# Attention maxima: turned by VectorE and laid out by two transfers instead of transposed by TensorE, with a new order of steps

## The chip, the cores and the metric

The kernel runs on one core of a Trainium2 chip. The core has TensorE (matrix products, written to PSUM), VectorE, ScalarE and GpSimd (element-wise work), SyncE (which here only asks for transfers), and 16 DMA engines that move data between DRAM and SBUF. The metric is the device time of one execution in microseconds (us); less is better.

## The reference

Four transformer layers act one after the other on x, 16 samples of 256 tokens by 256 features, in float32. Layers 0, 2 and 3 are whole: self attention, cross attention to a context of 120 rows, and an MLP. Layer 1 has cross attention alone. All have 16 heads of 16 features. The part that matters here is the softmax inside each attention:

```
def _attend(q, k, v):
    attn = jnp.einsum('bhnd,bhsd->bhns', q, k) * SCALE
    attn = jax.nn.softmax(attn, axis=-1)
    o = jnp.einsum('bhns,bhsd->bhnd', attn, v)
    B, _, N, _ = q.shape
    return o.transpose(0, 2, 1, 3).reshape(B, N, D)
...
x = x + g_sa * x_sa          # self attention, projected and gated
x = x + x_ca                 # cross attention
h = jax.nn.gelu(xm @ fc1_w + fc1_b, approximate=True)
x = x + g_ff * x_ff          # MLP
```

A softmax needs the maximum of every row of scores (one for each query and head) before the exponentials.

## The kernel before

Everything of x stays in SBUF. A job is one part of a layer for one sample, and is cut into steps. A list of words gives the order in which all engines go through the steps: a word such as `F.S0` names a part and a step, and each engine, in its own in-order queue, does what its part of each step is and waits on semaphores for the rest. A step with `.d` marks where VectorE (and GpSimd and SyncE) take their share when it isn't at TensorE's place.

The parts: P makes q, k and v of a self attention, F is the self attention, A its projection; R makes q, k and v of a cross attention, G is the cross attention, B its projection; E is the MLP. A leading `1` is layer 1; `p`, `f`, `c`, `e` are the same parts for another sample. A turn handles each part once, each for another sample (`AHEAD`). Turns 3 to 21 follow `WITH_L1` and also hold layer 1's cross attention (its G steps in turns 6 to 21, 16 jobs); turns 22 to 46 follow `TURN` and are called plain turns here. `START` and `TAIL` are the first and last stretch. There are 48 self attentions and 64 cross attentions, 112 in all.

One attention goes like this. `S` steps (four for F, two for G) write scores with queries on the partitions into `score`, a tile of four PSUM banks of which there is only one, and VectorE reduces each to row maxima (L978). `X` is VectorE's: it writes the negated maxima in two parts, a rounded one and its remainder, into `max_parts` (L987, L990), 8 used columns in each 32. `M` turns them: TensorE transposes the two 128 by 128 tiles into a slot of the ring (three PSUM banks shared by all projections, transposes and MLP steps; called from L1294, recorded at L1144), and ScalarE copies them to `max_t` (L1106). `T` steps write the scores again, keys on the partitions (L1309), add the negated maxima by a product with the selector `sel` (L1314), and ScalarE takes exponentials (L1117). `PV` multiplies by v (L1340) and `O` turns and normalizes on VectorE (L1000 to L1011). Every S and every T must wait until the one before it has left `score`.

In a timeline `score<-k_G,q_G` is an S step of a cross attention, `score<-q_F,k_F` with `score<-max_t_F,sel` a T step of a self attention, `ring<-ident,max_parts_G` is M, `w_proj` is A.PR, `w_cp` or `room` with `o_t_B` is B.PR, `w_fc,h_t` is F20 or F21 of E.

Of the kernel before, what the change touches and what calls it, by code (L numbers as in the profile page):

```python
# [47 lines left out]

TURN = """
F.S0 f.O1 f.PV3 E.H0  # L50
F.S1 P.V E.RES E.H1 P.V.d
F.S2 P.LN E.H2
F.S3 E.H3 p.N P.gld A.PR F.X A.PR.d
G.S0 F.M B.PR B.PR.d R.C
G.S1 E.F20a E.F20b G.X
F.T0 E.F20b.d R.N P.Q e.N G.M R.A
F.T1 e.A p.A P.Q.d P.K F.PV0
G.T0 c.NC P.RES F.PV1 P.K.d
P.ld R.LN e.LN F.O0 R.RES G.O0
G.T1 E.gld c.AC P.ST R.KV R.KV.d E.F21a G.O1 G.PV0  # L60
F.T2 R.Q G.PV1
F.T3 E.F21b E.F21b.d F.PV2 R.Q.d c.ld
""".split()
WITH_L1 = """
F.S0 f.PV3 E.H0
F.S1 1R.C P.V P.V.d P.LN
F.S2 P.gld E.H1 f.O1 E.H2
F.S3 F.X 1R.LN E.RES E.H3
1G.S0 A.PR F.M A.PR.d
1G.S1 1G.X B.PR E.F20a  # L70
G.S0 E.F20b 1G.M B.PR.d
G.S1 E.F21a
1G.T0 1R.RES E.F20b.d P.Q e.N
1G.T1 R.N e.A P.Q.d 1G.PV0 R.RES G.X 1G.O0 P.K
F.T0 E.F21b 1G.PV1
F.T1 G.M F.PV0 P.K.d R.A
P.ld 1R.Q E.F21b.d
G.T0 F.PV1 1G.O1 R.C p.N p.A 1R.KV 1R.Q.d F.O0
G.T1 G.PV0 1R.KV.d G.O0 R.LN 1B.PR 1p.N 1p.NC
F.T2 G.PV1 G.O1 R.Q E.gld R.Q.d P.RES  # L80
F.T3 R.KV P.ST 1p.AC 1R.ld 1B.PR.d F.PV2 c.ld 1p.A R.KV.d e.LN
# [3 lines left out]
W0.v Z0.ZT Z0.ZC P0.N P0.ld P0.A Z0.ZM Z0.ZX W0.cpb W0.proj Z0.ZL P0.LN Z0.ZA W0.raw Z1.ZL P2.ld W0.fc1 P0.Q  # L85
P1.ld W0.self P0.Q.d Z1.ZA P0.K Z0.ZS0 P0.K.d Z1.ZC Z2.ZL Z2.ZA W0.cross P1.N Z0.ZG Z1.ZM Z1.ZX
F0.S0 P1.A
F0.S1 P0.V P0.V.d
F0.S2 P1.LN Z0.ZS1 Z2.ZC
F0.S3 Z2.ZG Z3.ZL Z2.ZS1 F0.X Z2.ZM Z2.ZX F0.M  # L90
F0.T0 P2.N Z3.ZC R0.ld P1.Q Z3.ZA P1.Q.d F0.PV0
F0.T1 P1.K Z2.ZS0
F0.T2 P1.K.d Z3.ZM F0.PV1 P1.V
F0.T3 P3.ld F0.PV2 F0.O0 Z3.ZG
F1.S0 W0.fc2 R0.C P1.V.d
F1.S1 P5.ld P2.A F0.PV3 W0.v2
F1.S2 F0.O1
F1.S3 P2.LN P0.RES P0.gld F1.X A0.PR A0.PR.d F1.M
F1.T0 R0.N Z3.ZX R0.RES P2.Q P2.Q.d R1.ld
F1.T1 P2.K R0.A P3.N R0.LN P2.K.d F1.PV0 P2.V F1.PV1  # L100
F1.T2 Z3.ZS1 R0.Q P2.V.d
F1.T3 F1.O0 R0.KV P3.A
F2.S0 P1.RES W1.l1 F1.PV2 R2.ld R0.KV.d W0.cp
F2.S1 R0.Q.d
F2.S2 F1.PV3 F1.O1
F2.S3 A1.PR F2.X P4.ld
# [2 lines left out]
F2.T0 G0.X P1.gld R1.C P3.Q G0.M
F2.T1 P3.K  # L110
G0.T0 R1.N P3.Q.d P3.K.d R1.A F2.PV0 R1.LN F2.PV1 P4.N
G0.T1 F2.O0 R1.Q G0.O0 G0.PV0
F2.T2 Z3.ZS0 R1.Q.d G0.O1 P2.RES G0.PV1
F2.T3 P4.A R1.KV R1.KV.d R1.RES R3.ld P2.gld F2.PV2
# [1285 lines left out]
```

## Time and profile before

| | us |
|---|---|
| median of 3 runs | 2577.09 |
| lowest and highest | 2574.03, 2577.36 |
| the profiled execution | 2577.71 |
| its span, first to last instruction | 2575.9 |
| TensorE busy | 2479.3 |
| VectorE busy | 1858.5 |
| ScalarE busy | 1274.0 |
| GpSimd busy | 467.2 |

Busy times are sums over the whole span; an engine that is busy for less may still be the one that another waits for at a given place. The granted clock is TensorE's share of its full speed.

### The profile page before, as it was taken

Reading aid. Unit: us, or ns where it says so; the run is one execution under the profiler, and the core shown is the slowest. Engines: PE = TensorE matmul, PEld = TensorE weight load, DVE = VectorE, ACT = ScalarE, POOL = GpSimd, SP = SyncE. Lnnn points to the kernel's source line nnn. Section 1 sums busy time; section 2 is a strip of 40 time slices with the busy share of each in tenths; the row PEclk is TensorE's granted clock in tenths of the full one; section 3 lists DMA queues with packets and bytes.
Section 4 is the critical chain, followed back from the end, with each engine's and each line's share of the span. In section 5 each row is a group of like instructions: output and inputs, shape, how many; then the busy total and the mean of one; then the engine's idle time right before and its main releaser. Section 6 shows DMA issues by size and latency. Waiting matters only on the chain.

```text
span 2575.9 us, 66165 instructions
## 1 busy us (share of the span) xinstructions
PE 2479.3 (96%) x27466; PEld 1848.3 (72%) x27466; DVE 1858.5 (72%) x3532; ACT 1274.0 (49%) x1810; POOL 467.2 (18%) x510
## 2 busy tenths in 40 slices
...
GB/s 188 129 93 78 78 74 74 74 80 87 83 77 76 90 81 96 77 101 68 56 76 74 56 76 74 62 96 78 80 107 60 82 84 78 78 66 80 82 33 42
DMA packets 236749, 207.56 MB, mean 81 GB/s; under 512 B 87682, under 2 KB 222020, under 8 KB 236452
## 3 DMA queue, kind: packets, MB, share of 16 engines
...
## 4 chain that ended last, share of the span: by engine, by line
PE 79%; DVE 12%; issue 3%; ACT 3%; SPq 2%; DMA 1%; POOL 1%; DVEq 0%; POOLq 0%; ACTq 0%
PE o_acc L1340 11%; PE score L1287 10%; PE ring L1371 10%; PE ring L1248 10%; PE ring L1362 10%; PE score L1309 8%; PE ring L1352 6%; DVE row_max_F L978 5%; DVE row_max_G L978 5%; PE ring L1144 4%; PE ring L1256 3%; PE score L1314 3%; PE ring L1268 2%; ACT probs L1117 2%; PE ring L1271 2%
## 5 line engine op out<-in xcount | busy, mean ns | idle before, releaser
L1117 ACT ACTIVATE probs<-score 120x2048 f32<-120x2048 f32 (+1 forms) x320 | 601.6, 1880 | 374.8 <-PE score L1314 368.0
L978 DVE TENSOR_REDUCE row_max_F<-score 128x8 f32<-128x2048 f32 x192 | 438.7, 2285 | 103.3 <-PE score L1287 102.8
L1371 PE MATMUL ring<-w_fc,h_t 128*128 128x256 f32 x1536 | 368.9, 386 | 1.0 <-ACT h_t L1128 1.0
L1362 PE MATMUL ring<-x_t_E,w_fc 128*128 128x256 f32 x1536 | 368.3, 386 | 0.0
L978 DVE TENSOR_REDUCE row_max_G<-score 128x16 f32<-128x1920 f32 x128 | 276.1, 2157 | 116.8 <-PE score L1287 116.8
L1128 ACT ACTIVATE h_t<-ring,cols 128x256 f32<-128x256 f32 x384 | 160.7, 470 | 341.1 <-PE ring L1362 341.0
L1362 PEld LDWEIGHTS ring<-x_t_E,w_fc 128*128 128x128 f32 x1536 | 280.8, 190 | 59.3 <-issue 20.3
L1000 DVE STREAM_TRANSPOSE o_turned<-o_acc 128x512 f32<-128x512 f32 x224 | 159.9, 714 | 220.3 <-PE o_acc L1340 220.3
L1371 PEld LDWEIGHTS ring<-w_fc,h_t 128*128 128x128 f32 x1536 | 282.5, 190 | 46.3 <-ACT h_t L1128 1.4
L1340 PE MATMUL o_acc<-probs,v_self 128*17 128x256 f32 x3072 | 204.3, 384 | 0.0
L793 POOL TENSOR_TENSOR x<-x,gated 128x256 f32<-128x256 f32 x96 | 70.3, 733 | 723.1 <-DVE gated L1032 723.1
L1248 PE MATMUL ring<-x_t_P,w_qk 128*128 128x256 f32 x768 | 197.8, 403 | 1.2 <-ACT x_t_P L1068 1.2
L1309 PE MATMUL score<-q_F,k_F 32*128 32x256 f32 x3072 | 166.6, 303 | 8.9 <-ACT probs L1117 5.7
L1309 PEld LDWEIGHTS score<-q_F,k_F 32*128 32x128 f32 x3072 | 119.3, 184 | 75.2 <-issue 55.7
L1248 PEld LDWEIGHTS ring<-x_t_P,w_qk 128*128 128x128 f32 x768 | 143.9, 197 | 35.2 <-issue 8.4
L1287 PEld LDWEIGHTS score<-k_F,q_F 32*128 32x128 f32 x3072 | 106.4, 188 | 84.2 <-DVE row_max_F L978 42.0
L1287 PE MATMUL score<-k_F,q_F 32*128 32x256 f32 x3072 | 146.3, 307 | 21.4 <-DVE row_max_F L978 18.5
L1287 PEld LDWEIGHTS score<-k_G,q_G 32*128 32x128 f32 x4096 | 125.3, 187 | 52.4 <-DVE row_max_G L978 28.0
L1287 PE MATMUL score<-k_G,q_G 32*128 32x120 f32 x4096 | 142.9, 277 | 14.8 <-DVE row_max_G L978 12.0
L787 POOL TENSOR_TENSOR x<-x,gated 128x512 f32<-128x512 f32 x48 | 60.8, 1267 | 423.0 <-DVE gated L1019 423.0
L1340 PE MATMUL o_acc<-probs,v_ctx 120*17 120x256 f32 x2048 | 135.5, 382 | 0.0
L1099 ACT ACTIVATE q_parts<-ring,cols 128x256 fp32r<-128x256 f32 x224 | 94.0, 472 | 80.9 <-PE ring L1248 78.9
...
## 6 DMA issues: line engine op xcount, KB each, us to landing
q_G<-q_parts SPq DMA_DIRECT2D x256, 128.0 KB, 2.1
q_F<-q_parts SPq DMA_DIRECT2D x192, 128.0 KB, 2.1
k_F<-k_parts SPq DMA_DIRECT2D x96, 256.0 KB, 2.5
k_F<-k_parts SPq DMA_DIRECT2D x192, 128.0 KB, 2.2
k_G<-k_parts SPq DMA_DIRECT2D x128, 120.0 KB, 2.2
k_G<-k_parts SPq DMA_DIRECT2D x256, 60.0 KB, 1.9
gate_now_P<-gate_rows SPq DMA_DIRECT2D x48, 256.0 KB, 3.2
gate_now_E<-gate_rows SPq DMA_DIRECT2D x48, 256.0 KB, 3.4
```

The costliest lines, as they stand in the source:

```text
L978: nc.vector.tensor_reduce(dst, src, AX.X, ALU.max).then_inc(row_max_ready[r].sem, 1)
L1000: nc.vector.transpose(o_turned[:, :, :, :].rearrange("p i b d -> p (i b d)"), o_acc[:, :])\
L1117: nc.scalar.activation(probs[v % 2][0:keys, :, :], score[0:keys, :].rearrange("p (h q) -> p h q", h=2 * GROUPS), ACT.Exp, scale=SCALE).the ...
L1128: last = nc.scalar.activation(h_t[:, c, :], ps[:, c % 2 * NT:(c % 2 + 1) * NT], ACT.Gelu_apprx_tanh, bias=col(m, "fc1", c))
L1144: return nc.tensor.transpose(dst, src, ident[0:rows_in, 0:rows_in])
L1248: last = mm(ps[:, c * NT:(c + 1) * NT], weight[:, k, at + c * P:at + (c + 1) * P], buffer(x_t, r, m, n)[:, k, :], start=k == 0, stop=k == ...
L1287: last = mm(score[:, col0:col0 + width], q_now[at, c, e, tile * P:(tile + 1) * P].bitcast(F32R), k_now[at, two, c, e, :].bitcast(F32R), st ...
L1309: mm(score[0:keys, g * BANK + e * NT:g * BANK + (e + 1) * NT], k_now[at, two, c, e, tile * P:tile * P + keys].bitcast(F32R), q_now[at, c, ...
L1340: last = mm(o_acc[32 * j:32 * j + HD + 1, i * NT:(i + 1) * NT], v_head, probs[v % 2][0:keys, 2 * j + i, :], start=tile == 0 and (i == 0 or ...
L1352: last = mm(ps[:, t * D:(t + 1) * D], buffer(o_t, r, m, n)[:, k, t * P:(t + 1) * P], weight[:, k, :], start=k == 0, stop=k == KC - 1)
L1362: last = mm(ps[:, c % 2 * NT:(c % 2 + 1) * NT], w_fc1[:, k, c * P:(c + 1) * P], buffer(x_t, r, m, n)[:, k, :], start=k == 0, stop=k == KC - 1)
L1371: last = mm(ps[:, 0:D], h_t[:, k, t * P:(t + 1) * P], w_fc2[:, k, :], start=k == 0, stop=k == MC - 1)
```

## The change

M is no longer a step of TensorE and ScalarE. `max_parts` is packed (64 columns for both tiles instead of 256, no zeros between). X gets a third operation on VectorE, which turns `max_parts` in squares of 32 by 32 into `max_turned`. Then GpSimd asks for two transfers: one in X, from `max_turned` to a DRAM tensor `max_rows` of 32 rows by 256 queries, and one in M, from there to all four groups of 32 partitions of `max_t`. T waits for the second. The selector's ones stand at another row in each group, since each group now holds all 32 rows. M doesn't take a ring slot any more, so that the slots of all later steps shift.

```
+        max_rows = {r: nc.dram_tensor(f"max_rows_{r}", [32, NT], F32, kind="Internal").ap() for r in "FG"}
...
-        max_parts = {r: sb(f"max_parts_{r}", [P, TT, P]) for r in "FG"}
+        max_parts = {r: sb(f"max_parts_{r}", [P, TT, GROUPS, PAIRS, 2]) for r in "FG"}
+        max_turned = {r: sb(f"max_turned_{r}", [P, TT, 32]) for r in "FG"}
...  (GpSimd)
+                elif step == "X":
+                    pool.wait_ge(max_turned_ready[r].sem, max_turned_ready[r].after(m, n))
+                    if max_laid[r].order[m, n] > 0:
+                        pool.wait_ge(max_laid[r].sem(m, n), max_laid[r].after(m, n) - 16)
+
+                    pool.dma_start(max_rows[r].rearrange("h (t a q) -> a h t q", t=TT, a=4), max_turned[r][:, :, :])\
+                        .then_inc(max_written[r].sem(m, n), 16)
+                elif step == "M":
+                    pool.wait_ge(max_written[r].sem(m, n), max_written[r].after(m, n))
+                    t_psum[r].wait_before(pool, m, n)
+                    pool.dma_start(max_t[r][:, :], max_rows[r].unsqueeze(0).to_broadcast([GROUPS, 32, NT]))\
+                        .then_inc(max_laid[r].sem(m, n), 16)
...  (VectorE, X)
+                    dve.wait_ge(max_parts_ready[r].sem, max_parts_ready[r].after(m, n))
+                    if max_written[r].order[m, n] > 0:
+                        dve.wait_ge(max_written[r].sem(m, n), max_written[r].after(m, n) - 16)
+                    nc.vector.transpose(max_turned[r][:, :, :].rearrange("p t h -> p (t h)"),
+                                        max_parts[r][:, :, :, :, :].rearrange("p t g c e -> p (t g c e)"))\
+                        .then_inc(max_turned_ready[r].sem, 1)
...  (ScalarE)
-                elif step == "M":
-                    act.wait_ge(m_psum[r].sem, m_psum[r].after(m, n))
-                    t_psum[r].wait_before(act, m, n)
-                    nc.scalar.activation(max_t[r][:, :].bitcast(F32R), ps[:, 0:NT], ACT.Identity)\
-                        .then_inc(max_t_ready[r].sem, 1)
...  (TensorE)
-                elif step == "M":
-                    pe.wait_ge(max_parts_ready[r].sem, max_parts_ready[r].after(m, n))
-                    for t in range(TT):
-                        last = transpose(ps[:, t * P:(t + 1) * P], max_parts[r][:, t, :], P)
-                    last.then_inc(m_psum[r].sem, 1)
...  (TensorE, T0)
-                        pe.wait_ge(max_t_ready[r].sem, max_t_ready[r].after(m, n))
+                        pe.wait_ge(max_laid[r].sem(m, n), max_laid[r].after(m, n))
```

The lists `TURN`, `WITH_L1` and `START` have a new order; `TAIL` differs in where one gate is loaded. Two words of `WITH_L1`:

```
-1G.S1 1G.X B.PR E.F20a
+1G.S1 P.gld B.PR.d 1R.C E.F20a 1G.X 1G.M
```

TensorE, in a turn with layer 1, from layer 1's first S step to its first T step. Before:

```order
909 L1287 MATMUL score<-k_G,q_G 128x120 x32
910 L1352 MATMUL ring<-w_proj,o_t_A 128x256 x4
911 L1144 MATMUL ring<-ident,max_parts_F 128x128 x2
912 L1287 MATMUL score<-k_G,q_G 128x120 x32
913 L1352 MATMUL ring<-w_cp,o_t_B 128x256 x4
914 L1371 MATMUL ring<-w_fc,h_t 128x256 x4
915 L1287 MATMUL score<-k_G,q_G 128x120 x32
916 L1371 MATMUL ring<-w_fc,h_t 128x256 x4
917 L1144 MATMUL ring<-ident,max_parts_G 128x128 x2
918 L1287 MATMUL score<-k_G,q_G 128x120 x32
919 L1371 MATMUL ring<-w_fc,h_t 128x256 x4
920 L1309 MATMUL score<-q_G,k_G 120x256 x8
```

The same place of TensorE's list after the change:

```order
873 L1299 MATMUL score<-k_G,q_G 128x120 x32
874 L1359 MATMUL ring<-w_proj,o_t_A 128x256 x4
875 L1359 MATMUL ring<-w_cp,o_t_B 128x256 x4
876 L1299 MATMUL score<-k_G,q_G 128x120 x32
877 L1158 MATMUL ring<-ident,x_hat_C 128x120 x2
878 L1378 MATMUL ring<-w_fc,h_t 128x256 x4
879 L1299 MATMUL score<-k_G,q_G 128x120 x32
880 L1378 MATMUL ring<-w_fc,h_t 128x256 x4
881 L1158 MATMUL ring<-ident,room 128x120 x2
882 L1299 MATMUL score<-k_G,q_G 128x120 x32
883 L1378 MATMUL ring<-w_fc,h_t 128x256 x4
884 L1316 MATMUL score<-q_G,k_G 120x256 x8
```

B.PR (`w_cp`) has moved ahead of the second S step, both pairs of transposes of maxima are gone, and two context transposes (`x_hat_C`, `room`) now stand here.

GpSimd from self attention's addition to x (L787 before, L789 after) on in such a turn. Before:

```order
164 L787 TENSOR_TENSOR x<-x,gated 128x512
165 L783 TENSOR_TENSOR x<-x,room 128x512
166 L793 TENSOR_TENSOR x<-x,gated 128x256
167 L768 TENSOR_TENSOR rstd_E<-var_eps_E,minus_half 128x2
168 L768 TENSOR_TENSOR rstd_R<-var_eps_R,minus_half 128x2
169 L783 TENSOR_TENSOR x<-x,cp_bias 128x512
```

After (L802 is the transfer of X, L807 that of M, L770 the root for a norm, L795 and L789 additions to x):

```order
310 L789 TENSOR_TENSOR x<-x,gated 128x512
311 L802 DMA max_rows_G<-max_turned_G 4x64x32
312 L807 DMA max_t_G<-max_rows_G 128x1x256
313 L802 DMA max_rows_F<-max_turned_F 4x64x32
314 L795 TENSOR_TENSOR x<-x,gated 128x256
315 L770 TENSOR_TENSOR rstd_E<-var_eps_E,minus_half 128x2
316 L807 DMA max_t_F<-max_rows_F 128x1x256
317 L770 TENSOR_TENSOR rstd_R<-var_eps_R,minus_half 128x2
318 L802 DMA max_rows_G<-max_turned_G 4x64x32
319 L807 DMA max_t_G<-max_rows_G 128x1x256
```

The two transfers of layer 1 follow each other at once, and the root and the addition of E stand behind them.

VectorE in a plain turn, from the maxima of a cross attention's S steps on, before:

```order
2100 L978 TENSOR_REDUCE row_max_G<-score 128x16
2101 L1024 TENSOR_TENSOR x<-ring,x 128x512
2102 L978 TENSOR_REDUCE row_max_G<-score 128x16
2103 L987 TENSOR_SCALAR max_parts_G<-row_max_G 128x8x4
2104 L990 SCALAR_TENSOR_TENSOR max_parts_G<-row_max_G,max_parts_G 128x8x4
2105 L1032 TENSOR_TENSOR gated<-ring,gate_now_E 128x256
2106 L817 BN_STATS stats_R<-x 128x6 x2
2107 L822 BN_AGGR mean_var_R<-stats_R 128x2 x2
2108 L825 TENSOR_SCALAR var_eps_R<-mean_var_R 128x2
2109 L817 BN_STATS stats_E<-x 128x6 x2
2110 L822 BN_AGGR mean_var_E<-stats_E 128x2 x2
2111 L825 TENSOR_SCALAR var_eps_E<-mean_var_E 128x2
```

The same place of VectorE's list after the change:

```order
2559 L994 TENSOR_REDUCE row_max_G<-score 128x16 x2
2560 L1043 TENSOR_TENSOR x<-ring,x 128x512
2561 L833 BN_STATS stats_E<-x 128x6 x2
2562 L838 BN_AGGR mean_var_E<-stats_E 128x2 x2
2563 L841 TENSOR_SCALAR var_eps_E<-mean_var_E 128x2
2564 L1000 TENSOR_SCALAR max_parts_G<-row_max_G 128x32
2565 L1003 SCALAR_TENSOR_TENSOR max_parts_G<-row_max_G,max_parts_G 128x32
2566 L1009 STREAM_TRANSPOSE max_turned_G<-max_parts_G 128x64
2567 L833 BN_STATS stats_R<-x 128x6 x2
2568 L838 BN_AGGR mean_var_R<-stats_R 128x2 x2
2569 L841 TENSOR_SCALAR var_eps_R<-mean_var_R 128x2
2570 L849 TENSOR_SCALAR x_hat_E<-x,mean_var_E,rstd_E 128x256 x2
```

The preparation of the maxima of G now stands behind B's addition and E's statistics, and has the turning (L1009) as its third operation.

## Rows read from the trace of the kernel before

**Rows 1.** Stretches: length, busy us of each engine, PE clock, DMA share, GB/s.

```profile
0.00:193.00 193.00, 135.44 (x1470) 93.36 (x1471) 119.38 (x241) 57.80 (x74) 22.70 (x35) 0.84 0.42 137
193.00:2400.00 2207.00, 2182.74 (x24492) 1630.90 (x24491) 1650.55 (x3117) 1138.63 (x1623) 412.57 (x440) 1.00 0.25 78
```

**Rows 2.** Groups by form: out<-in, shapes, xcount, then busy us, mean ns, idle before.

```profile
L1000 DVE STREAM_TRANSPOSE o_turned<-o_acc 128x512 f32<-128x512 f32 x224 | 159.9, 714 | 220.3 <-PE o_acc L1340 220.3
...
L1144 PE MATMUL ring<-ident,max_parts_G 128*128 128x128 f32 x128 | 25.6, 281 | 0.0
```

**Rows 3.** TensorE in a turn with layer 1: start, length, [idle before].

```profile
797.91 1.11 PE L1287 MATMUL score<-k_G,q_G 32*128 32x120 f32 x32
798.95 1.99 PE L1352 MATMUL ring<-w_proj,o_t_A 128*128 128x256 f32 x8
...
801.36 1.11 PE L1287 MATMUL score<-k_G,q_G 32*128 32x120 f32 x32 [0.19 <-DVE row_max_G L978]
...
806.05 1.11 PE L1287 MATMUL score<-k_G,q_G 32*128 32x120 f32 x32
...
809.49 1.11 PE L1287 MATMUL score<-k_G,q_G 32*128 32x120 f32 x32 [0.19 <-DVE row_max_G L978]
...
812.87 0.50 PE L1309 MATMUL score<-q_G,k_G 32*120 32x256 f32 x8 [0.34 <-DVE row_max_G L978]
...
815.82 0.38 PE L1309 MATMUL score<-q_G,k_G 32*120 32x256 f32 x4
```

**Rows 4.** Timeline of VectorE and ScalarE in the same turn.

```profile
802.52 2.16 DVE L978 TENSOR_REDUCE row_max_G<-score 128x16 f32<-128x1920 f32 x1 [0.62 <-PE score L1287]
...
809.36 0.68 DVE L1024 TENSOR_TENSOR x<-ring,x 128x512 f32<-128x512 f32 x1
...
813.89 1.88 ACT L1117 ACTIVATE probs<-score 120x2048 f32<-120x2048 f32 x1 [4.17 <-PE score L1314]
```

**Rows 5.** TensorE's timeline, one plain turn.

```profile
1981.69 1.11 PE L1287 MATMUL score<-k_G,q_G 32*128 32x120 f32 x32
...
1985.13 1.11 PE L1287 MATMUL score<-k_G,q_G 32*128 32x120 f32 x32
...
1989.82 0.51 PE L1309 MATMUL score<-q_F,k_F 32*128 32x256 f32 x8
...
1992.88 0.51 PE L1309 MATMUL score<-q_F,k_F 32*128 32x256 f32 x8
...
1996.70 0.50 PE L1309 MATMUL score<-q_G,k_G 32*120 32x256 f32 x8
```

**Rows 6.** TensorE's timeline, two places of an earlier turn.

```profile
763.92 0.44 PE L1144 MATMUL ring<-ident,max_parts_G 128*128 128x128 f32 x2
764.28 1.06 PE L1340 MATMUL o_acc<-probs,v_self 128*17 128x256 f32 x16
...
769.09 0.42 PE L1144 MATMUL ring<-ident,context 120*128 120x120 f32 x2
769.35 0.83 PE L1268 MATMUL ring<-context_t,room 128*128 128x120 f32 x6
```

**Rows 7.** Transfers: out<-in, xcount, KB each, median us from issue to landing.

```profile
k_G<-k_parts SPq DMA_DIRECT2D x128, 120.0 KB, 2.2
k_G<-k_parts SPq DMA_DIRECT2D x256, 60.0 KB, 1.9
...
gate_now_E<-gate_rows SPq DMA_DIRECT2D x48, 256.0 KB, 3.4
...
gate_rows<-h_t SPq DMA_DIRECT2D x6, 32.0 KB, 2.1
...
v_bias<-in_L_xcond_b_qkv_dram SPq DMA_DIRECT2D x1, 128.0 KB, 4.3
```

**Rows 8.** Timeline before the last cross attention's first T step.

```profile
2527.62 0.20 DVE L990 SCALAR_TENSOR_TENSOR max_parts_G<-row_max_G,max_parts_G 128x32 fp32r<-128x32 f32 x1
...
2528.96 0.38 PE L1309 MATMUL score<-q_G,k_G 32*120 32x256 f32 x4 [0.57 <-ACT max_t_G L1106]
```

More of the change, by code:

```diff
@@ L49 @@
 TURN = """
[L50 to L62, printed above, removed]
+F.S0 f.PV3 f.O1 E.H0
+F.S1 E.RES P.V E.H1 P.V.d
+F.S2 p.N E.H2 P.LN
+F.S3 E.H3 A.PR F.X A.PR.d
+G.S0 F.M R.C B.PR
@@ L63 @@
+G.S1 B.PR.d E.F20a E.F20b
+F.T0 e.N G.X R.N e.A G.M P.Q R.A P.Q.d
+F.T1
+P.ld F.PV0 E.F20b.d P.K
+G.T0 R.RES c.NC P.K.d F.O0 R.LN e.LN G.O0 F.PV1
+G.T1 R.KV G.PV0 E.F21a E.gld
+F.T2 R.KV.d R.Q G.PV1
+F.T3 G.O1 E.F21b c.AC c.ld p.A P.gld P.RES F.PV2 R.Q.d E.F21b.d P.ST
 """.split()
 WITH_L1 = """
[L65 to L69, printed above, removed]
-1G.S1 1G.X B.PR E.F20a
-G.S0 E.F20b 1G.M B.PR.d
+F.S0 E.RES 1R.RES f.PV3 E.H0
+F.S1 P.LN P.V P.V.d
@@ L82 @@
+G.T0 F.PV1 R.LN 1R.KV e.A 1p.N p.N F.O0 1R.Q.d
+G.T1 R.RES G.PV0 1R.KV.d G.O0 e.LN 1B.PR
+P.ld E.gld 1B.PR.d
+F.T2 P.RES G.O1 G.PV1 R.Q p.A P.ST
+F.T3 R.Q.d 1p.A R.KV R.KV.d c.ld 1p.AC F.PV2
 """.split()
 START = """
[L85 to L106, printed above, removed]
@@ L107 @@
-G0.S0 F2.M
-G0.S1 A1.PR.d P3.LN
[L109 to L114, printed above, removed]
+P0.ld W0.raw P0.N P0.A Z0.ZT Z0.ZC Z0.ZM Z0.ZX Z0.ZL Z0.ZA W0.proj P1.ld Z1.ZL W0.fc1 W0.self P0.LN Z1.ZA P0.Q
+P1.N P0.Q.d Z0.ZG P0.K P0.K.d W0.v Z0.ZS0 Z2.ZA W0.cpb Z2.ZL Z0.ZS1 Z1.ZM Z1.ZC Z1.ZX P1.A
+F0.S0 P0.V P0.V.d P2.ld
+F0.S1
+F0.S2 P1.LN Z2.ZC Z3.ZL W0.cross
```

75 lines of the change are left out of this document (47 added, 28 removed).

## The prediction

> **What bounds the kernel now.** I read the table of stretches first. Between 193 and 2400 us TensorE is busy 2182.74 of 2207 us at full granted clock, and idle for 24; another 58 idle us lie before 193, where the mean granted clock is 0.84 [rows 1]. So TensorE's work sets the pace, and a change that takes work from it looks like plain gain. The groups by form say how much: the 128 transposes of the cross attention's maxima cost TensorE 25.6 us, 0.20 each [rows 2]; with the 96 of the self attention, 45 us. From the start of such a pair to the start of what follows it is 0.36 us in one place (763.92 to 764.28 [rows 6]). 112 pairs take then between 22 us (one transpose's 0.20 each, if the rest overlaps) and 46; I take 0.3 each, 33 us.
>
> Then the timeline, to see whether TensorE would be free to use that time. It would often not be. There is one score tile: a score step S writes it, VectorE takes its maxima, and only then may the next step write it. In a turn with layer 1, four cross-attention S steps start at 797.91, 801.36, 806.05 and 809.49, and the first T step at 812.87; three of these starts wait 0.19, 0.19 and 0.34 us for VectorE [rows 3]. The maxima of the S at 801.36 run from 802.52 for 2.16 us [rows 4]; adding the handover, one S cannot follow another in less than 3.44 us. For T, with ScalarE's exponentials (813.89 for 1.88), the distance is 2.95 us (812.87 to 815.82) [rows 3, 4]. A removed pair inside a gap at its floor gives nothing: the idle time that the pair filled only comes to light. "99% busy" hides that.
>
> **What the change removes, adds and moves, one steady turn at a time.** I write each gap as the larger of its TensorE work and its floor, in the new order.
>
> Plain turns (numbers 22 to 46, 25 of them). Before, the two G score steps start 1981.69 and 1985.13, 3.44 apart: exactly the floor, with the F pair inside [rows 5]. After, the pair is gone and the floor stays: gain 0. The first two F steps of T are 3.06 apart with the G pair between (1989.82, 1992.88) [rows 5]; the floor of 2.95 leaves 0.11. The other gaps hold the same work. 25 x 0.11 = 2.8 us.
>
> Turns with layer 1 (16 with all of its steps). Before, 797.91 to 812.87 is 14.96 us. After, both projections (A.PR, B.PR) follow the first S: 1.04 for the S (797.91 to 798.95) and 1.83 for each projection, 4.70 in all [rows 3]. Then a context transpose and F20a make 3.2, under the floor: 3.44. Then VectorE must do B's addition (0.68) and prepare the maxima (about 0.2 twice, then the new turning) before it can take the next maxima [rows 4, 8]. The turning of 64 columns: a turning of 512 takes 0.714 us [rows 2] and an operation on 32 takes 0.20 [rows 8], so I take 0.24 for 64. That is 1.4 us where 1.2 are free (an S and its handover, 801.36 to 802.52): 3.64. The last gap is at the floor, 3.43. Sum 15.2, 0.25 more than before, although two pairs are gone, because two context transposes (0.26 each, 769.09 to 769.35 [rows 6]) have come in and the waits for VectorE are longer. Outside it, the third pair goes (0.36, 763.92 to 764.28 [rows 6]), and of the context transposes' 0.52 some 0.39 is won where they stood, since one stood in a gap that meets its floor without it. Net 0.25 - 0.36 - 0.39 = -0.50 a turn, 8 us; for the three turns before layer 1 joins I take 1 us. The steady gain is thus 11.8 us, not 33. The turning is 112 x 0.24 = 27 us more on VectorE, which has 556 idle us of 2207 [rows 1]; where that cover is missing it is in the 3.64 above. ScalarE's 112 copies go at no gain: the T gaps wait for its exponentials, not for them.
>
> **The new path from X to T.** The maxima now go VectorE, a transfer to DRAM, a transfer back to four copies, then T, with GpSimd asking for both. The lead is counted from the end of the turning to where T would start anyway.
> - Layer 1, counted from the second S: its maxima are there at 3.4 (1.16 + 2.16 and a handover), B's addition ends at 4.1, the turning at 4.85. T0 stands at 3.44 + 3.64 + 3.43 = 10.5: a lead of 5.65 us.
> - Plain turns, G: VectorE has B's addition and E's statistics ahead, for which I take 1.2, so the turning ends 6.0 after the second G step. T0 is 4.69 + 2.95 + 3.82 = 11.46 after it (1985.13 to 1989.82; floor; 1992.88 to 1996.70) [rows 5]: 5.46 us.
> - F in both kinds of turn has over 8 us, and G in a layer-1 turn 11, by the same adding up of gaps.
>
> No row shows a transfer that GpSimd asks for, so I bound it by those that SyncE asks for [rows 7]. The least is 1.9 us (60 KB), so a chain of two with 0.2 of handovers is at least 4.0. From above, 3.4 for the write (as much as 256 KB take one way), 4.3 for the read (a broadcast of 128 KB) and the 0.2: 7.9. Nearest to the write is the 32 KB one to gate_rows, 2.1, plus 0.3 for being cut into 256 pieces of 128 bytes, 16 for each engine (k_G's 120 KB have 8 pieces more on each engine than its 60 KB: 2.2 against 1.9). Nearest to the read is the broadcast gate_rows to gate_now_E, 3.4. Chain: 2.1 + 0.3 + 3.3 + 0.2 = 5.9 us, where 3.3 allows a little for half the size. What GpSimd adds I leave in the range.
>
> Late by 0.25 us in 16 turns: 4. Late by 0.44 in 25: 11. TensorE runs its list in order, so all behind T0 waits too and nothing later gives it back: 15 us. GpSimd has idle time enough (412.57 of 2207 us busy [rows 1]); behind the waiting second transfer stand its add and the E or R root, none due within 2 us, so I cost that at 0, and at 1 us a turn if the cover is gone. SyncE's queue only meets two more small transfers a job on the same engines, busy for a quarter of the time [rows 1]: 0.
>
> Ends. In the last cross attention T0 starts at 2528.96, released by ScalarE; the second preparing operation begins at 2527.62 for 0.20 [rows 8]. Turned at 2528.05, plus 5.9, T0 is at 2533.9: 4.9 later. The one before has other waits behind it that hide a part; between 0 and 4.9, I take 2.8. At the start the first two self attentions have only their neighbours' steps as cover, which leaves between 0 and 4.9 each; I take 2. With saved pairs -1.5, the ends cost 10. The start's order is otherwise new, and 58 idle us lie there; I give it 0, with 8 either way.
>
> Sum: 2577.7 (the profiled execution, 0.6 over the median of 2577.09, so I need no correction) - 11.8 + 15 + 10 = 2591.
>
> **Two rules of the Trainium skill.** The row says 2.1 us for a small write with 16 rows on each side [rows 7]. "DMA: Bandwidth & Descriptors", section "Why a DMA increments its semaphore by 16 and not by 1", says that a transfer runs on the largest number of engines up to 16 that divides the slowest dimension of both sides; here that dimension is 4 on one side of both transfers, so they would run on 4. No row here has such a shape. It is the second rival below. The same page, section "Anatomy of one DMA", fits a GpSimd transfer as about 2.0 us plus its bytes at 436 GB/s; as an estimate from that page, the chain would be 4.6 us and the first rival holds. Against it stands the broadcast row of 3.4 us.
>
> **The rivals.**
> 1. The chain fits. For it: the least rows (1.9, 2.1) [rows 7] and two transfers under 5.4 us. Against: the read is a broadcast from DRAM and such rows are 3.4 and 4.3. The 15 us go, the ends cost 5: 2577.7 - 11.8 + 5 = 2571; with the start's 8 us, 2563 to 2577. Faster than before, or the same.
> 2. Few engines (slower, and by much). If each transfer is spread over 4 engines, the write puts 64 pieces on one instead of 16, the read 32 instead of 8. By k_G's rows 8 more pieces cost 0.3 us [rows 7], so 1.8 and 0.9 more: a chain of 8.6 us. T0 is late by 2.95 us in 16 turns and 3.14 in 25, 126 us, the ends cost 21: 2577.7 - 11.8 + 126 + 21 = 2713. For it: the uneven shapes of both transfers; against it, only that no row of the trace is slow in that way. It decides from a chain of 7 us on.
> 3. The score floor is softer than I think (VectorE's maxima start earlier), or the new start saves more: the 33 us come out nearly whole, 2577.7 - 33 + 15 + 10 = 2570, or with a chain that fits 2550. Against it stand the waits of 0.19 and 0.34 us [rows 3].
>
> **How the numbers follow.** Forecast (chain 5.5 to 7 us; 2578 to 2635) 0.38. Chain fits 0.37. Few engines 0.17. Rest, of either sign, 0.08. A difference under 0.2%, 5 us, can't be told from none. Faster: 0.27 of the fit and 0.03 of the rest, 0.30. Same: 0.07 of the forecast, 0.10 of the fit, 0.02: 0.19. Slower: 0.31 + 0.17 + 0.03 = 0.51. The forecast's own range is 2578 to 2635. The whole range goes from 2562 (chain at its least, a better start) to 2676 (a chain of 7.9: 2.25 x 16 + 2.44 x 25 = 97, less 11.8, and the ends 13); rival 2 in its full size is left above it.
>
> **What would show it.** In the changed profile: no transposes of max_parts and no max_t copies; TensorE's busy time down by 40 to 46 us; S steps in the first half still 3.4 us apart with longer waits for row_max_G. The waits of TensorE's T steps for a DMA into max_t_G are the test: some 15 us in total in the forecast, near 0 in rival 1, over 100 in rival 2, and near 0 for max_t_F in all. The two transfers' times to landing give the chain directly. The forecast is wrong if these waits are small and the time is still over 2580, or if plain turns get shorter than 46.4 us.

## The result and the profile after

The changed kernel takes 2814.86 us (median of 4 runs, 2814.23 to 2823.96), the kernel before in the same session 2575.56 (2573.84 to 2577.36): a ratio of 1.0937, 95% interval 1.0913 to 1.0962. It is slower, as the larger chance said, but by 239 us where the forecast had 13, and far outside the range of 2562 to 2676. Its profiled execution has a span of 2813.6 us at a mean granted clock of 0.951 (before: 2575.9, 0.987).

Stages, cut where VectorE starts the first maxima of the self attentions 6, 22 and 47 (before: 300.87, 1266.48, 2433.11; after: 332.30, 1353.84, 2649.58):

| us | before | after | difference | forecast |
|---|---|---|---|---|
| start to job 6 | 300.9 | 332.3 | +31.4 | +1 |
| 16 turns with layer 1 | 965.6 | 1021.5 | +55.9 (3.5 a turn) | -4 |
| 25 plain turns | 1166.6 | 1295.7 | +129.1 (5.2 a turn) | +8 |
| rest | 142.8 | 164.0 | +21.2 | +8 |

The stretches that answer to [rows 1] first (length, busy us of each engine, granted clock, DMA share, GB/s), then those of the turns:

```profile
0.00:193.00 193.00, 122.68 (x1240) 83.40 (x1241) 106.66 (x212) 44.88 (x57) 24.00 (x35) 0.79 0.41 129
193.00:2400.00 2207.00, 2051.88 (x22461) 1515.01 (x22457) 1531.97 (x2984) 1023.14 (x1399) 570.73 (x592) 0.97 0.28 80
...
332.00:1354.00 1022.00, 957.94 (x10932) 707.48 (x10930) 749.70 (x1472) 485.47 (x665) 277.13 (x284) 0.97 0.29 83
1354.00:2650.00 1296.00, 1202.75 (x12662) 887.26 (x12654) 851.04 (x1637) 585.57 (x801) 319.60 (x336) 0.96 0.26 75
```

TensorE is idle for 155 us between 193 and 2400 instead of 24, and its clock is no longer full. Its waits in the 16 turns with layer 1, and then in the plain turns (us in total, times, longest), name what it waits for:

```profile
PE score L1316 <- DMA max_t_G<-max_rows_G: 48.2, 16, 3.8
PE score L1299 <- DVE row_max_G L994: 6.2, 32, 0.3
PE score L1299 <- DVE row_max_F L994: 5.9, 12, 0.7
...
PE score L1316 <- DMA max_t_G<-max_rows_G: 79.6, 25, 5.1
PE score L1299 <- DVE row_max_G L994: 6.0, 25, 0.2
PE score L1316 <- DMA max_t_F<-max_rows_F: 5.1, 7, 1.1
```

One long wait a turn, always a cross attention's first T step (layer 1's own in the turns that have it), 3.0 and 3.2 us in the median; those of F in the plain turns sum to 5.1. The transfers behind it, which no row of before showed (KB, median us from issue to landing; [rows 7] had 2.1 and 3.4 for the nearest ones), and GpSimd's and VectorE's own part (us busy, mean ns):

```profile
max_t_G<-max_rows_G POOLq DMA_DIRECT2D x64, 128.0 KB, 4.7
max_t_F<-max_rows_F POOLq DMA_DIRECT2D x48, 128.0 KB, 4.1
max_rows_G<-max_turned_G POOLq DMA_DIRECT2D x64, 32.0 KB, 3.4
max_rows_F<-max_turned_F POOLq DMA_DIRECT2D x48, 32.0 KB, 3.3
```

```profile
L802 POOL DMA_DIRECT2D max_rows_G<-max_turned_G x64 | 82.8, 1294 | 81.5 <-DVE max_turned_G L1009 77.9 <-issue 1.4
L807 POOL DMA_DIRECT2D max_t_G<-max_rows_G x64 | 46.2, 722 | 143.3 <-DMA max_rows_G<-max_turned_G 127.9 <-PE score L1321 15.5
L1009 DVE STREAM_TRANSPOSE max_turned_G<-max_parts_G 128x64 f32<-128x64 f32 x64 | 15.7, 245 | 2.5 <-DVE max_parts_G L1003 0.3
```

One plain turn, which answers to [rows 5], in the timelines of TensorE, VectorE and GpSimd (start, length, [idle before]), put together here in order of time:

```profile
1991.44 1.11 PE L1299 MATMUL score<-k_G,q_G 32*128 32x120 f32 x32
...
1994.88 1.11 PE L1299 MATMUL score<-k_G,q_G 32*128 32x120 f32 x32 [0.24 <-DVE row_max_G L994]
...
2000.43 0.24 DVE L1009 STREAM_TRANSPOSE max_turned_G<-max_parts_G 128x64 f32<-128x64 f32 x1
...
2000.97 1.40 POOL L802 DMA_DIRECT2D max_rows_G<-max_turned_G  x1
...
2004.83 0.75 POOL L807 DMA_DIRECT2D max_t_G<-max_rows_G  x1 [1.69 <-DMA max_rows_G<-max_turned_G]
...
2010.12 0.70 PE L1316 MATMUL score<-q_G,k_G 32*120 32x256 f32 x8 [2.90 <-DMA max_t_G<-max_rows_G]
2010.55 0.48 PE L1321 MATMUL score<-max_t_G,sel 32*120 32x256 f32 x4
...
2012.51 1.06 PE L1158 MATMUL ring<-ident,x_hat_E 128*128 128x128 f32 x4
```

The two S steps stand 3.44 apart, as before and as predicted. Turned at 2000.67, asked for 0.30 later, the read 3.86 after that, T0 another 5.29 later: 9.45 us from the turning to T0, where 5.9 was forecast. Then a second cost. Eight products that take 0.50 elsewhere take 0.70, and four transposes 1.06, where the same ones take 0.60 in the kernel before and in e8 below. The stretches around it show the granted clock:

```profile
2005.00:2010.00 5.00, 2.22 (x16) 1.44 (x8) 1.94 (x7) 2.08 (x3) 3.06 (x4) 1.00 0.45 120
2010.00:2014.00 4.00, 3.88 (x40) 3.11 (x44) 0.00 (x0) 2.29 (x3) 0.00 (x0) 0.57 0.82 275
2014.00:2020.00 6.00, 6.00 (x72) 4.21 (x64) 3.23 (x7) 3.54 (x6) 0.00 (x0) 1.00 0.02 3
```

TensorE is busy 2.22 of 5 us, and for most of the 4 us after that it is granted the lower of its levels, 1.2 of 2.4 GHz (0.57 in the mean).

### The profile page after: what moved, and what is told of

Its sections match the earlier page's. It is cut to its first block, busy times and chain, and to the rows that moved or that the text cites. A ratio compares the mean times of both kernels' runs of the same rounds, so it can differ in the third digit from the quotient of the medians.

```text
span 2813.6 us, 66048 instructions
## 1 busy us (share of the span) xinstructions
PE 2537.2 (90%) x27242; PEld 1870.6 (66%) x27242; DVE 1869.0 (66%) x3647; ACT 1239.2 (44%) x1698; POOL 693.3 (25%) x732
## 4 chain that ended last, share of the span: by engine, by line
issue 30%; PE 27%; DMA 17%; SPq 9%; POOL 9%; DVE 7%; ACT 1%; POOLq 0%; DVEq 0%; ACTq 0%
DMA max_t_G<-max_rows_G 7%; PE ring L1260 6%; PE o_acc L1347 6%; PE score L1316 5%; PE ring L1378 3%; DMA gate_now_P<-gate_rows 3%; DMA max_rows_F<-max_turned_F 3%; POOL x L785 2%; DMA gate_now_E<-gate_rows 2%; SPq L667 2%; SPq L666 2%; SPq L665 2%; POOL max_rows_G L802 2%; PE ring L1158 2%; PE score L1321 2%
## 5 line engine op out<-in xcount | busy, mean ns | idle before, releaser
L1378 PEld LDWEIGHTS ring<-w_fc,h_t 128*128 128x128 f32 x1536 | 279.7, 190 | 55.5 <-issue 12.1
L785 POOL TENSOR_TENSOR x<-x,gate_now_P 128x512 f32<-128x512 f32 x48 | 64.2, 1337 | 805.4 <-DMA gate_now_P<-gate_rows 805.4
L1316 PE MATMUL score<-q_G,k_G 32*120 32x256 f32 x2048 | 125.8, 332 | 150.2 <-DMA max_t_G<-max_rows_G 145.4
L1316 PEld LDWEIGHTS score<-q_G,k_G 32*120 32x120 f32 x2048 | 91.3, 205 | 207.9 <-issue 197.6
L1347 PE MATMUL o_acc<-probs,v_self 128*17 128x256 f32 x3072 | 219.2, 406 | 0.0
L1260 PE MATMUL ring<-x_t_P,w_qk 128*128 128x256 f32 x768 | 216.1, 431 | 1.2 <-ACT x_t_P L1087 1.2
L1316 PE MATMUL score<-q_F,k_F 32*128 32x256 f32 x3072 | 169.6, 307 | 44.8 <-DMA max_t_F<-max_rows_F 28.2
L1260 PEld LDWEIGHTS ring<-x_t_P,w_qk 128*128 128x128 f32 x768 | 155.0, 212 | 47.7 <-issue 21.2
L865 DVE SCALAR_TENSOR_TENSOR q_parts<-ring,cols,q_parts 128x256 fp32r<-128x256 f32 x224 | 97.0, 474 | 105.2 <-ACT q_parts L1118 105.1
```

The costliest lines, as they stand in the source:

```text
L785: nc.gpsimd.tensor_tensor(x[n][:, :, :], x[n][:, :, :], bias, ALU.add).then_inc(x_biased[r].sem, 1)
L865: last = nc.vector.scalar_tensor_tensor(out=parts[:, 1, c, 0:width].bitcast(F32R), in0=src[:, c * width:(c + 1) * width], scalar=row_col(m ...
L1260: last = mm(ps[:, c * NT:(c + 1) * NT], weight[:, k, at + c * P:at + (c + 1) * P], buffer(x_t, r, m, n)[:, k, :], start=k == 0, stop=k == ...
L1316: mm(score[0:keys, g * BANK + e * NT:g * BANK + (e + 1) * NT], k_now[at, two, c, e, tile * P:tile * P + keys].bitcast(F32R), q_now[at, c, ...
L1347: last = mm(o_acc[32 * j:32 * j + HD + 1, i * NT:(i + 1) * NT], v_head, probs[v % 2][0:keys, 2 * j + i, :], start=tile == 0 and (i == 0 or ...
L1378: last = mm(ps[:, 0:D], h_t[:, k, t * P:(t + 1) * P], w_fc2[:, k, :], start=k == 0, stop=k == MC - 1)
```

## The experiments

Each ran beside the kernel before. "Way" is the time from the end of VectorE's turning to the start of T0 where T0 waits (median over a stage's cross attentions, layer-1 turns first); "fits" means that in the turns T0 waits for no transfer, or for at most three short ones. First the table, then the runs.

| run | us, ratio (95% interval) | start | layer-1 turn | plain turn | rest | way |
|---|---|---|---|---|---|---|
| before (profiled) | 2575.9 | 300.9 | 60.35 | 46.67 | 142.8 | |
| after (profiled) | 2813.6 | 332.3 | 63.85 | 51.83 | 164.0 | 8.3, 9.1 |
| e1 old order | 2812.4, 1.0923 (1.0904 to 1.0942) | 349.1 | 68.05 | 48.32 | 162.9 | F 8.8, G 9.0 (plain) |
| e2 new order, TensorE turns | 2607.1, 1.0123 (1.0108 to 1.0138) | 303.2 | 61.37 | 47.09 | 144.0 | |
| e3 maxima of the job before | 2581.7, 1.0027 (1.0018 to 1.0036) | 311.7 | 59.59 | 46.67 | 146.6 | no wait |
| e4 one hop, SyncE | 2576.5, 0.9999 (0.9990 to 1.0009) | 303.8 | 59.72 | 46.66 | 151.3 | fits |
| e5 two hops, SyncE | 2646.7, 1.0279 (1.0264 to 1.0294) | 314.5 | 60.93 | 47.91 | 157.0 | 6.9, 6.9 |
| e6 two hops, even shapes | 2597.9, 1.0087 (1.0072 to 1.0102) | 314.9 | 59.71 | 46.78 | 156.2 | fits |
| e7 one hop, GpSimd | 2583.6, 1.0034 (1.0020 to 1.0049) | 302.4 | 59.72 | 46.73 | 155.5 | fits |
| e8 filler | 2765.9, 1.0737 (1.0714 to 1.0760) | 329.9 | 62.79 | 50.29 | 166.1 | 8.5, 9.2 |
| e9 small read | 2629.5, 1.0211 (1.0197 to 1.0225) | 319.8 | 60.14 | 47.48 | 160.7 | 6.2, 6.4 |
| e10 old order, one hop | 2588.7, 1.0050 (1.0037 to 1.0062) | 313.5 | 60.07 | 46.52 | 149.1 | fits |
| e11 mixed | 2569.4, 0.9976 (0.9967 to 0.9985) | 302.6 | 59.69 | 46.66 | 141.1 | fits |
| e12 even broadcast | 2658.5, 1.0323 (1.0309 to 1.0338) | 323.4 | 60.88 | 48.05 | 160.4 | 6.6, 6.9 |

**Order or path? (e1, e2)** e1 has the tables TURN, WITH_L1, START and TAIL of before, and all else of the change.

> The turns and first turns of before, with the new way of the maxima (VectorE's turning and the two transfers for which GpSimd asks). Theory A, latency: in the changed kernel each transfer takes 3.3 to 5 us from issue to landing and the way from the turning to T0 is 8.4 to 9.5 us where 5.9 was forecast, so TensorE waits 174 us at the first T step and runs at half clock for some us behind each wait; the old order has about the same distances, so 2750 to 2880 us. Theory B, the new order costs by itself (GpSimd's and SyncE's queues stand behind the late gate load in it): 2590 to 2640 us.

e2 is the kernel before with the tables of the change, and one place moved:

```diff
-G.S1 E.F21a
-1G.T0 e.N P.Q F.M R.N G.X
+G.S1 F.M E.F21a
+1G.T0 e.N P.Q R.N G.X
```

> The new order of turns, with the maxima turned by TensorE as before (M of the self attention is put behind the next S step in turns with layer 1, since the ring of PSUM tiles allows no other place). Theory A, latency: within 15 us of before, 2562 to 2592. Theory B, the order costs by itself: over 2700.

e1 came as theory A has it. The old order with the new path is as slow as the changed kernel, so it isn't the new order that costs the 240 us. The order decides where the wait falls: 100.1 us of it in the turns with layer 1 and 41.7 in the plain ones, against 48.2 and 84.7. In e1's layer-1 turns GpSimd's own list costs as well: it asks for G's write 2.7 us after the turning in the median (0.3 in the plain turns), since additions to x stand ahead. e2 misses both bands (2607), nearer to theory A's: the new order costs 31 us when TensorE turns the maxima, 16.4 of them in the layer-1 turns, where TensorE now waits 19.1 us for VectorE's max_parts_G. It was made for the other path.

**The latency alone (e3).** All work and all transfers stay, but T uses the maxima of the job before (so the output is not the reference's).

```diff
-        max_t = {r: sb(f"max_t_{r}", [P, NT]) for r in "FG"}
+        max_t = {r: [sb(f"max_t_{r}{i}", [P, NT]) for i in range(2)] for r in "FG"}
-                        pe.wait_ge(max_laid[r].sem(m, n), max_laid[r].after(m, n))
+                        pe.wait_ge(max_laid[r].sem(m, n), max(16, max_laid[r].after(m, n) - 16))
```

> The changed kernel with two tiles for max_t of each kind: a T step uses the maxima that the transfers laid for the job before, so that all work and all transfers stay and only the wait for them goes (the exponentials get a smaller scale so that they stay finite; the output is not the reference's). Theory A, latency: the forecast's steady gain of 11.8 us comes to light, 2555 to 2580 us, and no drop of the granted clock. Theory B, GpSimd's queue or the order costs: over 2650.

TensorE's waits in its 41 turns (312 to 2432) hold no transfer any more:

```profile
PE score L1299 <- DVE row_max_G L994: 12.3, 57, 0.3
PE score L1316 <- DVE row_max_G L994: 5.5, 16, 0.3
PE score L1299 <- DVE row_max_F L994: 2.5, 6, 0.6
PE score L1316 <- ACT probs L1131: 1.3, 2, 0.9
```

All the steady loss is gone, and the granted clock is 1.00 in both stages. GpSimd still stands 645.9 us at P.RES for the gate load in this run, and it costs nothing. The turns are 59.59 and 46.67 us. The total, 2581.7, is just above its band all the same, since the start (311.7) and the rest (146.6) stay 10.8 and 3.8 us longer than before.

**One hop (e4, e7).** The squares go straight into max_t, and the selecting matrix takes every fourth row:

```diff
+                    dst = max_t[r][0:P:4, :].rearrange("h (t a q) -> h t a q", t=TT, a=4)
+                    for a4 in range(4):
+                        sp.dma_start(dst[:, :, a4, :], max_turned[r][32 * a4:32 * (a4 + 1), :, :])
```

> The changed kernel with one hop in place of two: SyncE asks for four transfers of 8 KB from the turned squares straight into every fourth partition of max_t, none of DRAM and none by GpSimd. Theory A, latency: the hop takes 2.2 to 3 us, under the distances of 5.5 us, so T0 never waits: 2555 to 2580 us. Theory B: over 2650. If small pieces and few engines are the cost and not the number of hops, the hop takes 4 us or more and still fits: the same time, but the row shows it.

> The one-hop kernel (four transfers of 8 KB from the turned squares into every fourth partition of max_t), asked for by GpSimd in place of SyncE. If GpSimd's fixed part is some 2 us a chain and 0.7 to 1.3 us an issue: four issues of 0.7 to 1.3 and 2 to 2.5 us for the last to land, 5 to 7.5 us, so 2580 to 2680 us, against 2576 with SyncE asking. If what counts is the number of hops alone: 2576, as with SyncE.

e4's time is in its band, and no T0 of the 41 turns waits. But the hop is longer than the 2.2 to 3 us expected: each transfer lands 1.8 us after its issue, the four issues follow one another (0.61 us each on SyncE's queue), and where it shows T0 comes 4.5 us after the first (2487.64 to 2492.17). That still fits under the distance of 5.7. e7's time, 2583.6, is just inside the band of its first theory, and yet neither theory holds: GpSimd's issues take 0.56 us each and land in 1.7, and the way where it shows, at the end, is 3.8 us, where 5 to 7.5 was expected; it is shorter than with SyncE (4.0 and 4.6). Of the 4.5 us that e7's profiled execution is longer than e4's, 4.2 lie in the rest; what holds them I did not find. What is left of the loss is at the end: in e4 the last two T0 wait 8.4 us together.

**Who asks, and in which shape? (e5, e6, e9, e12)** e5 moves the change's two transfers, unaltered, into SyncE's queue.

> The changed kernel with the same two transfers over the same DRAM tiles, asked for by SyncE in place of GpSimd, at the same places of the order. Theory GpSimd: the prediction priced them by SyncE's rows, and what is long is what GpSimd adds; then the write lands in 2.1 to 2.5 us and the read in 3.3 to 3.6, the way from the turning to T0 is some 5.9 us as forecast, and the time 2585 to 2610 us. Theory transfers: two hops over DRAM in these small pieces are slow whoever asks (few engines): way over 8 us, 2750 us or more.

Neither theory holds. In a plain turn (timelines of VectorE, SyncE's queue and TensorE):

```profile
1456.94 0.24 DVE L1009 STREAM_TRANSPOSE max_turned_G<-max_parts_G 128x64 f32<-128x64 f32 x1
...
1457.21 0.52 SPq L681 DMA_DIRECT2D max_rows_G<-max_turned_G  x1
...
1459.54 0.52 SPq L686 DMA_DIRECT2D max_t_G<-max_rows_G  x1
...
1463.85 0.50 PE L1316 MATMUL score<-q_G,k_G 32*120 32x256 f32 x8 [0.92 <-DMA max_t_G<-max_rows_G]
```

The read follows the write by 2.33, as forecast (2.1 + 0.3), where GpSimd's takes 3.7. But T0 comes 4.3 after the read's issue (4.5 in the median), a full microsecond over the 3.3 that was forecast. Leaving GpSimd out takes 1.4 us off the way in the layer-1 turns and 2.2 in the plain ones, and leaves it too long.

e6 keeps GpSimd and gives both transfers an outermost dimension that 16 divides:

```diff
-pool.dma_start(max_rows[r].rearrange("h (t a q) -> a h t q", t=TT, a=4), max_turned[r][:, :, :])
+pool.dma_start(max_rows[r], max_turned[r][:, :, :].rearrange("p t q -> p (t q)"))
-pool.dma_start(max_t[r][:, :], max_rows[r].unsqueeze(0).to_broadcast([GROUPS, 32, NT]))
+pool.dma_start(max_t[r][0:P:4, :].rearrange("h (t a q) -> h t a q", t=TT, a=4),
+               max_rows[r].rearrange("(a h) (t q) -> h t a q", a=4, t=TT))
```

> The changed kernel, GpSimd asking, two hops, but both transfers with even shapes: the DRAM tile stands as the turned squares do, 128 rows of 256 bytes (no dimension of 4 outermost), and the read takes 32 rows once into every fourth partition, 32 KB in place of 128. Theory few engines (rival 2 of the prediction): each transfer falls to 2 to 2.5 us, the way is under 6 us, 2580 to 2620 us. Theory GpSimd: the write stays at 3.2 us or more, the read at 3.3 or more, the way 7 to 8 us: 2670 to 2760 us.

e9 has the change's write and a read of 32 KB (`max_t[r][0:P:4, :]` from `max_rows[r]`), e12 the same write and a read of 128 KB with 32 outermost:

```diff
-pool.dma_start(max_t[r][:, :], max_rows[r].unsqueeze(0).to_broadcast([GROUPS, 32, NT]))
+pool.dma_start(max_t[r][:, :], max_rows[r].unsqueeze(1).to_broadcast([32, GROUPS, NT]))
```

> The changed kernel with its write as it is (dimension 4 outermost on the DRAM side), and a read of 32 rows of 1 KB once into every fourth partition, 32 KB in place of 128. The write should stay at 3.3 to 3.7 us to the read's issue by both theories (its shape and pieces are unchanged); the read falls to 2.0 to 2.4 us. The way is 0.3 + 3.7 + 2.4 = 6.4 us, 0.7 over the distance of 5.7: 41 x 0.7 = 29 us, the clock's share for some, over the 2598 us of the run with two even shapes: 2620 to 2665 us.

> As the run with the small read, but the read again lays 128 KB, 1 KB pieces, into all partitions: row h into partitions 4h to 4h+3, so that 32 and not 4 is the outermost dimension. Theory few engines: the read lands in 2.2 to 3.0 us, and the time is within 20 us of the run with the small read. Theory bytes: 4 us or more as in the changed kernel, the way 8.2 us, and 2740 us or more.

The transfers of e6, then of e9, then of e12 (KB, median us to landing):

```profile
max_rows_G<-max_turned_G POOLq DMA_DIRECT2D x64, 32.0 KB, 1.8
max_t_G<-max_rows_G POOLq DMA_DIRECT2D x64, 32.0 KB, 2.2
```

```profile
max_rows_G<-max_turned_G POOLq DMA_DIRECT2D x64, 32.0 KB, 3.6
max_t_G<-max_rows_G POOLq DMA_DIRECT2D x64, 32.0 KB, 2.0
```

```profile
max_t_G<-max_rows_G POOLq DMA_DIRECT2D x64, 128.0 KB, 2.5
...
max_rows_G<-max_turned_G POOLq DMA_DIRECT2D x64, 32.0 KB, 3.6
```

The pair of after and e12 is the cleanest: same bytes, same 1 KB pieces, same engine asking. The outermost dimension is 32 in place of 4 (with it the order of the pieces changes), and the read takes 2.5 us in place of 4.7. e6's write takes 1.8 in place of 3.4, and GpSimd's time to ask for it falls from 1.29 to 0.61. Its pieces grow too, from 128 to 256 bytes, but small pieces alone are not it: e6's read has 256 pieces of 128 bytes and lands in 2.2. So of e6's two theories the shape stands (2597.9 is in its band), and no fixed price of GpSimd's.

What the shape does can be seen in the start, within the third read into max_t_F, where no other transfer is under way. The stretch in after, then in e12:

```profile
146.50:147.50 1.00, 0.00 (x0) 0.00 (x0) 0.97 (x3) 0.00 (x0) 0.79 (x1) 0.50 0.27 99
144.50:145.15 0.65, 0.00 (x0) 0.00 (x0) 0.65 (x1) 0.00 (x0) 0.61 (x1) 0.50 0.51 202
```

The 128 KB come at 99 GB/s with 0.27 of the 16 DMA engines busy (4.3 on average), and at 202 GB/s with 0.51 (8.2). So fewer engines at work is what makes the change's read slow. For the write this is not shown.

e9 came as expected (2629). e12's read landed as its first theory has it, but the time is 29 us over e9, more than the 20 allowed: its 41 waits are 51.2 us against 32.2, the start is 3.6 longer, and in the turns TensorE is busy for 6.2 us more (2100.7 against 2094.5), because the clock fell a few times, as the next run explains.

The rule that the prediction named, "DMA: Bandwidth & Descriptors" of the Trainium skill, section "Why a DMA increments its semaphore by 16 and not by 1", says how many engines carry a transfer, not what that costs. The two stretches agree with it: fewer engines at 4 outermost than at 32, though no row gives their exact number. For the write the price hangs on who asks as well: with the same shape SyncE's read can follow its write by 2.3 us, GpSimd's by 3.7. The same page's section "Anatomy of one DMA" puts a GpSimd transfer at about 2.0 us plus its bytes at 436 GB/s, as an estimate 2.1 us for 32 KB and 2.3 for 128. The even shapes are near it (1.8 to 2.5); those with 4 outermost are not (3.4 and 4.7).

**The clock (e8).** Work with no use, put into the wait:

```diff
+                    if step == "F21a" and self_order[m, n] < 18:
+                        for k in range(MC // 2):
+                            mm(ps[:, 0:D], h_t[:, k, t * P:(t + 1) * P], w_fc2[:, k, :], start=k == 0, stop=k == MC // 2 - 1)
...
+                    twice = 2 if r == "P" and step == "K" and self_order[m, n] >= 23 else 1
+                    for c in twice * [*range(KC)]:
```

> The changed kernel with TensorE work added just ahead of the late T0 steps, its result thrown away: F21a's eight products run twice in the turns with layer 1 (18 times), the self attention's K twice in the plain turns (25), 1.99 us each, 86 us in all. Theory clock: behind each wait of some 3 us TensorE runs at half clock for some us, which costs 1.2 to 1.5 us beside the wait; the added work lies in the wait and keeps it to 1 us, so the clock stays up: 2745 to 2790 us, faster than the changed kernel in spite of more work. Theory wait alone: the extra work is hidden and the time the same, 2805 to 2825 us. If there is no slack in the waits: up to 86 us more.

TensorE does 344 products more, 86 us at full clock, and the kernel is 49 us faster than the changed one, in the band of theory clock. Its stages, and TensorE in a plain turn:

```profile
330.00:1335.00 1005.00, 965.02 (x11060) 717.26 (x11054) 751.26 (x1471) 484.71 (x665) 275.81 (x284) 1.00 0.30 85
1335.00:2592.00 1257.00, 1206.99 (x12854) 900.03 (x12850) 850.08 (x1637) 581.77 (x800) 319.50 (x336) 1.00 0.27 77
```

```profile
1923.20 0.50 PE L1317 MATMUL score<-q_G,k_G 32*120 32x256 f32 x8 [1.48 <-DMA max_t_G<-max_rows_G]
...
1924.60 0.60 PE L1158 MATMUL ring<-ident,x_hat_E 128*128 128x128 f32 x4
```

The way is as long as in the changed kernel, but behind a wait of 1.48 us the eight products take 0.50 again and the transposes 0.60. In the 41 turns the waits for the transfers fall from 132.9 to 63.2 us. TensorE's busy time there rises by 12 us only, with 82 us of added work in it, so that some 70 us of slow work are gone.

The mean of 1.00 hides a few exceptions. In after the clock fell behind 37 of the 41 long waits (2.0 us and more). Behind the shorter ones it fell in 3 turns of e8 and in 4 of e12, each time after a wait of 1.6 to 2.0 us, while others as long were followed by full clock; in e9, with 0.8 us on average, in none. One of e12's, a stretch and then TensorE's timeline in it, where the eight products of w_qk take 3.48 us in place of 1.99:

```profile
900.00:904.00 4.00, 4.00 (x28) 2.74 (x24) 1.22 (x7) 2.14 (x2) 3.00 (x4) 0.57 0.10 36
```

```profile
899.32 0.50 PE L1316 MATMUL score<-q_G,k_G 32*120 32x256 f32 x8 [1.87 <-DMA max_t_G<-max_rows_G]
...
900.22 3.48 PE L1260 MATMUL ring<-x_t_P,w_qk 128*128 128x256 f32 x8
```

**A better version (e10, e11).** e10 is e4 with the turns and first turns of before.

> The one-hop kernel with SyncE asking, in the turns and first turns of before (the end as in the changed kernel). If the old order is the better one once TensorE has no transposes of the maxima: its layer-1 turns are 60.0 us or less and its plain turns 46.0 to 46.5, 2565 us or less. If the gaps are at their floors in it, as the prediction reckons for both orders: turns of 60.4 and 46.5, 2580 to 2590 us with the ends.

(SyncE asks at the old order's M in place of its X there, since its queue stands at X otherwise.) e11 is e4 with the first turns of before (G0.X next to G0.M for the same reason), and in the tail F21a and F21b are taken from where they stood behind T1:

```diff
-G14.S1 G14.X E12.F20a R15.N E12.F20b E12.F20b.d G14.M R15.RES
+G14.S1 G14.X E12.F20a R15.N E12.F20b E12.F21a E12.F21b E12.F20b.d E12.F21b.d G14.M R15.RES
-G15.S1 E13.F20a E13.F20b G15.X G15.M
+G15.S1 E13.F20a E13.F20b G15.X G15.M E13.F21a E13.F21b
```

> A version meant to be faster than both: one hop asked for by SyncE, the turns of the change, the first turns of before, and in the end the two F21 products of one part each moved ahead of the last two cross attentions' T0, where the one-hop kernel waits 4.5 and 3.9 us. Start at turn 6 at 301 us in place of 304, tail 143 to 147 in place of 151: 2564 to 2571 us, 0.2 to 0.5% faster than before. If the start is ruled by something else and the moved products only move the waits: 2574 to 2578 us.

e10 is the second case of its expectation (2588.7, turns of 60.07 and 46.52): the old order is not the better one. The 41 turns of e10 together are 8.1 us under before, those of e4, with the change's order, 10.2; the old order has the better plain turn (46.52 against 46.66), the new the better layer-1 turn (59.72 against 60.07). Its start is 12.6 us longer than before. e11 is as hoped, 0.24% faster than before (interval 0.15 to 0.33%): the last two T0 wait 0.5 us each (before the move 4.5 and 3.9), and the rest is 141.1 us.

## Why the prediction was wrong

**The steady gain of 11.8 us: right in its size.** With a way that fits (e4) the 16 layer-1 turns give 10.0 us, 0.63 each (forecast 0.50), and the 25 plain ones 0.1 in all (forecast 2.8): 10.2. That the score tile's floor eats most of the 33 us was so. Rival 3 falls. Plain turns did not get under 46.4. In a layer-1 turn of e4 the first S to the first T takes 14.9 us where the forecast has 15.2, mainly because the gap with VectorE's preparation is 3.45 and not 3.64.

**The leads: right for G.** In e3 T0 stands 5.69 us after the turning, in plain turns (forecast 5.46) and for layer 1's own in its turns (5.65). F's, forecast as over 8 in both kinds, are 9.6 and 7.4 to 8.6; against a way of some 8.3 that left 5.1 us of waits in all the turns. The test that the prediction set for rival 2, over 100 us of waits for max_t_G, was met (145.4 in the whole run). The other, near 0 for max_t_F, was not: 28.2 us, 20.4 of them in the start.

**The chain of 5.9 us: the step that failed.** The prediction wrote "2.1 + 0.3" for the write and "3.3" for the read, by [rows 7] of transfers that SyncE asks for with 16 or more rows outermost. Measured 0.3 to the issue, 3.7 to the next, 4.3 (layer 1) or 5.1 (plain) to T0: 8.3 and 9.1 us. e5 splits the difference: the read was short by 1.2 us even when SyncE asks, the write by 1.3 because GpSimd asks in this shape; e12 and e6 show that the shape is what does it. In the plain turns GpSimd's read takes another 0.6 us (5.1 against e5's 4.5), which no run separates.

The prediction had few engines as its second rival, with 8.6 us, and from it late by 126 us in the turns; the waits there are 48.2 + 79.6 = 127.8. That this total comes out so near is in part luck: the rival's price holds whoever asks, and e5's write, in the same shape, took only 2.3. It gave the rival 0.17, with "no row of the trace is slow in that way" against it, though no row had the shape at all. That no row speaks for a rule is no evidence where no row could.

**What no case had: the clock.** The 41 turns together are 197.1 us over e3's (2317.3 against 2120.2), and the waits for the two transfers hold 132.9 (48.2 + 79.6 + 5.1). That leaves 64.2, and TensorE's busy time shows them: for the same instructions it is 2160.0 us in these turns, 67.1 more than in e3, 1.4 a layer-1 turn and 1.8 a plain one, at the lower level behind the waits. e8 takes them away by adding work. Hence the test "busy time down by 40 to 46" failed as well: over the whole run TensorE's busy time rose from 2479.3 to 2537.2. The test was too high by itself, though: in e3, without the waits, it is 2461.2, down by 18 and not by 40.

**The ends: 52.7 in place of 10.** In the start T0 of F waits 20.4 us in five places (longest 7.6), and in the rest 2.8, 8.3 and 8.2; the last two stand behind nothing that covers them, and were forecast late by 4.9 and less. In the start 10.8 us stay even without the wait for the maxima (e3), and 2.9 with one hop; the granted clock of the first 193 us is also lower, 0.79 against 0.84. Which of the start's steps hold them I did not separate.

**GpSimd's blocking at 0: right in the change's order,** by e3. (In the old order it was not, by e1.) The turning was right, 0.245 us (0.24).

The sum: -12.1 (e3's 41 turns) + 132.9 (waits) + 64.2 (the clock, as what is left over e3) + 52.7 (ends) = 237.7, as measured between the two profiled executions. Rival 2 with the clock and the ends as they were would have been 2713 + 64 + 32 = 2809.
